# A perceiver kernel: cross attentions that begin with keys and scores, with the order of the absorbed attention, the phase features, the wide loads and the final norm changed too

## The reference

```python
# L0, L1 cross attention: 16 heads of 16
Q, K, V = heads(query @ Wq + bq), heads(ctx @ Wk + bk), heads(ctx @ Wv + bv)
x = x + merge(softmax(Q K^T / 4) V) @ Wo + bo            # L1 clamps the scores
# L0 attention: q and k get features of a phase
a = softplus(t); amp = a / sqrt(mean(a*a over the head) + 1e-6)
features = amp * sin(pi*tanh(p)), amp * cos(pi*tanh(p))  # those of q times lambda
# L2 cross attention: 8 heads of 64; L3 cross attention: one head of 256
# L3 feed-forward (mixture of 8 experts, top 2), the last step of all
src = src + moe(src); x = x + norm2_w * src / sqrt(mean(src*src) + 1e-6)
```

## Time and profile before

| | |
|---|---|
| time, median of 3 runs | 2164.79 us (2161.39 to 2168.08) |
| profiled execution, its own time | 2166.26 us |
| its span | 2164.5 us |
| PE busy | 1633.4 us (75%) |
| DVE busy | 1021.2 us (47%) |
| ACT busy | 732.4 us (34%) |
| POOL busy | 479.7 us (22%) |
| L0_xattn from, L0_attn's phase features | 28.4, 262.1 to 337.2 |
| L1_xattn from, L2's absorbed attention | 675.8, 1250.9 to 1451.3 |
| L3_xattn prepared from, run from | 1740.5, 1761.7 |

### The profile page before, as it was taken

How to read it: one execution, slowest core, us unless ns; L and a number is a source line. 1 busy time by engine, 2 the same in 40 slices (tenths; PEclk the granted TensorE clock), 3 DMA queues, 4 the chain that set the end, 5 groups by cost and what they waited for, 6 DMA issues and landing times. The chain is left out here.

```text
span 2164.5 us, 54009 instructions
## 1 busy us (share of the span) xinstructions
PE 1633.4 (75%) x21983; PEld 1404.8 (65%) x21983; DVE 1021.2 (47%) x2154; ACT 732.4 (34%) x1682; POOL 479.7 (22%) x634
## 2 busy tenths in 40 slices
PE   5998635769986999764888478867388968877684
PEld 4887534659974777654777367864277946655573
DVE  5655484241117888336111446554855734344314
ACT  3554331123333555221323245542223322332121
POOL 3442242002213343100444121200001200010241
PEclk9999755569997999765999789997697979676797
DMA  4110000049972111003999612210100153000584
GB/s 141 53 51 23 4 0 3 4 172 343 346 266 85 51 47 28 5 3 114 304 298 306 239 52 83 78 49 0 42 24 30 39 184 114 4 2 13 176 283 166
DMA packets 89649, 228.61 MB, mean 106 GB/s; under 512 B 20008, under 2 KB 42792, under 8 KB 81904
## 3 DMA queue, kind: packets, MB, share of 16 engines
q1 hardware_dynamic: 81296, 203.49, 28.5%
q0 software_dynamic: 8160, 22.29, 3.1%
HBM read 210.34 MB, written 15.34 MB: 104 GB/s over the span
## 5 line engine op out<-in xcount | busy, mean ns | idle before, releaser
L2215 PEld LDWEIGHTS ps<-xt,w 128*128 128x128 f32 x1728 | 212.6, 197 | 10.2 <-issue 4.0
L2215 PE MATMUL ps<-xt,w 128*128 128x128 f32 x1728 | 214.3, 281 | 2.5 <-DVE xt L2396 2.1
L2253 ACT ACTIVATE g<-ps,b 128x128 f32<-128x128 f32 x340 | 122.5, 367 | 272.7 <-PE ps L2215 253.0
L2225 PE MATMUL ps<-w,g 128*128 128x256 f32 x864 | 206.9, 388 | 0.0
L2225 PEld LDWEIGHTS ps<-w,g 128*128 128x128 f32 x864 | 160.7, 194 | 19.2
L2273 POOL DMA_INDIRECT x<-rows,token x85 | 83.3, 980 | 293.0 <-DVEq L2372 264.2
L2278 POOL DMA_INDIRECT results<-y,dest x85 | 83.7, 985 | 283.7 <-DVE y L2409 223.8
L2396 DVE COPY xt<-ps 128x256 f32<-128x256 f32 x85 | 36.1, 425 | 229.8 <-PE ps L2205 181.6
L472 PE MATMUL ps<-x,w 128*128 128x512 f32 x408 | 112.0, 433 | 19.5 <-DVE x L610 19.5
L454 PE MATMUL ps<-consts_sb,z_sb 128*128 128x128 f32 x176 | 41.3, 406 | 110.1 <-DVE z_sb L598 110.0
L454 PEld LDWEIGHTS ps<-consts_sb,z_sb 128*128 128x128 f32 x176 | 32.9, 210 | 119.9 <-DVE z_sb L598 116.6
(11 more groups left out here) (403 smaller groups left out, 3673.7 us busy)
## 6 DMA issues: line engine op xcount, KB each, us to landing
w<-in_L_ffn_w SPq DMA_DIRECT2D x124, 512.0 KB
w<-in_L_ffn_w SPq DMA_DIRECT2D x46, 1024.0 KB
c<-in_ctx SPq DMA_DIRECT2D x96, 258.0 KB, 2.8
b<-in_w_L_ffn SPq DMA_DIRECT2D x62, 128.0 KB
rows<-in_w_L_xattn SPq DMA_DIRECT2D x32, 192.0 KB
rows<-in_w_L_xattn SPq DMA_DIRECT2D x8, 768.0 KB
c<-in_w_L_xattn SPq DMA_DIRECT2D x8, 514.0 KB
back<-results SPq DMA_DIRECT2D x16, 256.0 KB, 5.2
```

The lines of the kernel that those rows point to most:

```text
L2215: mm = nc.tensor.matmul(hidden_bank(par, h), b.w1[:, par, c, h * P:(h + 1) * P], b.xt[:, par, c, :], start=c == 0, stop=c == DC - 1)
L2225: mm = nc.tensor.matmul(k.ps[:, YB + par, 0:D], b.g[:, par, h, :], b.w2[:, par, h, :], start=h == 0, stop=h == HC - 1)
L2253: nc.scalar.activation(b.g[:, par, h, :], hidden_bank(par, h), func, bias=b.b1[:, par, h:h + 1]).then_inc(s.g_ready, 1)
```

## The change

Six edits. In L0 and L1 cross attention PE makes keys, values and scores of batch 0 before the product of the tails; POOL orders the tails' columns after batch 0's split, DVE takes the first maxima before the values and before round_context(2), and bo is added to x in `prepare`. In the absorbed attention add_tails of a batch stands in that batch, before the split of the queries. The phase features leave POOL: ACT folds by Abs and squares, DVE multiplies sine and cosine by the amplitude first and by the norm from PSUM last. The context loads of L3_xattn are waited for slot by slot in the stage that uses them, and queries(i + 2) stand before outputs(i - 1). The last mixture norms, adds and stores tile by tile; `store_output` is gone.

```diff
+    for dst, src, done in ahead:
+        sp.dma_start(dst, src).then_inc(done, 16)
...
+                if raised is not None:
+                    dve.wait_ge(s.norm_done, NT)
+                    nc.vector.tensor_tensor(src[:], src[:], spread(raised, NT, 1), ALU.add)
...
-                if ahead:
+                if m:
...
+                    else:
+                        pe.wait_ge(s.tail_ready, 1)
...
+            pe.wait_ge(s.w_split, 2)
+            keys_values(0, 0, ahead=False)
+            scores(0, 0)
             pe.wait_ge(s.t_ordered, 2)
             for c, t in ((0, b.t0), (1, b.t1)):
                 kr = P if c == 0 else DK - P
-                last = nc.tensor.matmul(k.ps[0:B, 7, 0:D], t[:], w.wv[0:kr, c, :], start=c == 0, stop=c == 1)
+                last = nc.tensor.matmul(k.ps[0:B, OB, 0:D], t[:], w.wv[0:kr, c, :], start=c == 0, stop=c == 1)
             last.then_inc(s.tail_done, 1)
-            pe.wait_ge(s.w_split, 2)
-            keys_values(0, 0, ahead=False)
-            pe.wait_ge(s.tail_ready, 1)
-            scores(0, 0)
-            pe.wait_ge(s.values_ready, 1)
...
+            split_context(0)
+            spread_queries(0, 0)
             for t, ordered in ((given.t0, b.t0), (given.t1, b.t1)):
                 nc.gpsimd.tensor_copy(ordered[:].rearrange("p (b t) -> p b t", b=BT),
                                       t[:].rearrange("p (t b) -> p b t", b=BT)).then_inc(s.t_ordered, 1)
                 pool.wait_ge(s.t_ordered, 1 if ordered is b.t0 else 2)
-            split_context(0)
-            spread_queries(0, 0)
...
             round_context(1)
+            maxima(0, 0)
+            take_values(0, 0)
             round_context(2)
             dve.wait_ge(s.tail_done, 1)
             dve.wait_ge(s.ones_set, 2)
-            nc.vector.tensor_tensor(b.vtail[:, :, 0:16], k.ps[0:B, 7, 0:D].rearrange("p (h d) -> p h d", d=16),
+            nc.vector.tensor_tensor(b.vtail[:, :, 0:16], k.ps[0:B, OB, 0:D].rearrange("p (h d) -> p h d", d=16),
                                     w.bv[0:B, :].rearrange("p (h d) -> p h d", d=16), ALU.add).then_inc(s.tail_ready, 1)
-            take_values(0, 0)
-            maxima(0, 0)
-            nc.vector.tensor_tensor(k.x[:], k.x[:], spread(w.bo, NT, 1), ALU.add).then_inc(s.x_ready, 1)
-            dve.wait_ge(s.x_ready, 1)
...
-                        if not (begin and j == 0):
-                            add_tails(n - 1, (j + 1) % 2, group if j else group - 1, (j - 1) % BT)
                         if not final:
                             maxima(n + 1, (j + 1) % 2)
                         if not (end and j >= 2):
                             round_context(n + 2, j % 2, 4 * it + 2 * gpar + j // 2 + 1)
                         if not final:
                             reciprocals(n + 1, (j + 1) % 2)
+                        add_tails(n, j % 2, group, j)
...
-                dve.wait_ge(s.amp_done, u + 1)
-                nc.vector.tensor_tensor(b.f[:, u], amp[:, u], amp[:, u], ALU.mult).then_inc(s.square_done, 1)
...
+            dve.wait_ge(s.amp_done, 2)
+            dve.wait_ge(s.lam_done, 1)
+            for done, t in ((s.sin_done, sn), (s.cos_done, cs)):
+                dve.wait_ge(done, 1)
+                for c in range(DC):
+                    nc.vector.scalar_tensor_tensor(t[:, 0, c], t[:, 0, c], b.lam[:, 1, c:c + 1], amp[:, 0, c],
+                                                   ALU.mult, ALU.mult).then_inc(s.scaled, 1)
+                dve.wait_ge(done, 2)
+                nc.vector.tensor_tensor(t[:, 1], t[:, 1], amp[:, 1], ALU.mult).then_inc(s.scaled, 1)
+            for u in range(2):
                 dve.wait_ge(s.root_done, u + 1)
                 nc.vector.reciprocal(b.rms[:, 1, u], b.rms[:, 0, u]).then_inc(s.recip_done, 1)
+            dve.wait_ge(s.scaled, 6)
             for u in range(2):
                 for q in range(4):
                     dve.wait_ge(s.wide_done, 4 * u + q + 1)
-                    part = amp[:, u, q // 2, (q % 2) * 512:(q % 2) * 512 + 512]
-                    nc.vector.tensor_tensor(part, part, k.ps[:, 4 * u + q, :], ALU.mult).then_inc(s.norm_done, 1)
-            dve.wait_ge(s.norm_done, 8)
-            dve.wait_ge(s.lam_done, 1)
-            for done, t in ((s.sin_done, sn), (s.cos_done, cs)):
-                dve.wait_ge(done, 2)
-                for c in range(DC):
-                    nc.vector.scalar_tensor_tensor(t[:, 0, c], t[:, 0, c], b.lam[:, 1, c:c + 1], amp[:, 0, c],
-                                                   ALU.mult, ALU.mult)
-            nc.vector.tensor_tensor(cs[:, 1], cs[:, 1], amp[:, 1], ALU.mult)
...
-            for u in range(2):
-                nc.scalar.activation(ph[:, u], ph[:, u], ACT.Tanh).then_inc(s.tanh_done, 1)
+            nc.scalar.activation(ph[:, 0], ph[:, 0], ACT.Tanh).then_inc(s.tanh_done, 1)
             for u in range(2):
                 act.wait_ge(s.abs_done, u + 1)
                 nc.scalar.activation(amp[:, u], amp[:, u], ACT.Exp, scale=-1.0).then_inc(s.exp_done, 1)
+            nc.scalar.activation(ph[:, 1], ph[:, 1], ACT.Tanh).then_inc(s.tanh_done, 1)
+            for u in range(2):
+                act.wait_ge(s.tanh_done, u + 1)
+                nc.scalar.activation(cs[:, u], ph[:, u], ACT.Abs).then_inc(s.fold_done, 1)
             for u in range(2):
                 act.wait_ge(s.plus_done, u + 1)
                 act.wait_ge(s.rest_done, u + 1)
                 nc.scalar.activation(b.f[:, u], b.f[:, u], ACT.Ln).then_inc(s.ln_done, 1)
-            act.wait_ge(s.tanh_done, 2)
             act.wait_ge(s.const_done, 2)
             for u in range(2):
                 nc.scalar.activation(sn[:, u], ph[:, u], ACT.Sin, scale=PI).then_inc(s.sin_done, 1)
+            act.wait_ge(s.amp_done, 1)
+            nc.scalar.activation(b.f[:, 0], amp[:, 0], ACT.Square).then_inc(s.square_done, 1)
             for u in range(2):
                 act.wait_ge(s.fold_done, u + 1)
                 nc.scalar.activation(cs[:, u], cs[:, u], ACT.Sin, bias=b.half[:, 0:1], scale=-PI).then_inc(s.cos_done, 1)
+            act.wait_ge(s.amp_done, 2)
+            nc.scalar.activation(b.f[:, 1], amp[:, 1], ACT.Square).then_inc(s.square_done, 1)
...
-        @block.gpsimd
-        def _(pool):
-            nc.gpsimd.memset(b.eps[:], 1e-6).then_inc(s.const_done, 1)
-            nc.gpsimd.memset(b.half[:], PI / 2).then_inc(s.const_done, 1)
-            for u in range(2):
-                pool.wait_ge(s.tanh_done, u + 1)
-                nc.gpsimd.tensor_scalar(cs[:, u], ph[:, u], 0.0, 2.0, ALU.max, ALU.mult).then_inc(s.rise_done, 1)
-                pool.wait_ge(s.rise_done, u + 1)
-                nc.gpsimd.tensor_tensor(cs[:, u], cs[:, u], ph[:, u], ALU.subtract).then_inc(s.fold_done, 1)
-            pool.wait_ge(s.norm_done, 8)
-            pool.wait_ge(s.sin_done, 2)
-            nc.gpsimd.tensor_tensor(sn[:, 1], sn[:, 1], amp[:, 1], ALU.mult)
...
+            pe.wait_ge(s.root_done, 2)
...
+            if finish is not None:
+                for t in range(NT):
+                    sp.wait_ge(s.finished, t + 1)
+                    sp.dma_start(k.out[:, t], k.x[:, t]).then_inc(k.stored, 16)
+                sp.wait_ge(k.stored, 16 * NT)
...
+            if finish is not None:
+                for t in range(NT):
+                    act.wait_ge(s.summed, (t + 1) * top)
+                    if t:
+                        act.wait_ge(s.squared, t)
+                    nc.scalar.activation(fin.square[:], into[:, t, :], ACT.Square, scale=1.0 / 16,
+                                         accum_out=fin.mean[:, t:t + 1]).then_inc(s.squared, 1)
+                    if t % 4 == 3:
+                        act.wait_ge(s.squared, t + 1)
+                        if t == 3:
+                            act.wait_ge(s.eps_set, 1)
+                        nc.scalar.activation(fin.root[:, t - 3:t + 1], fin.mean[:, t - 3:t + 1], ACT.Sqrt,
+                                             bias=fin.eps[:, 0:1]).then_inc(s.rooted, 1)
...
+                def scale(t):
+                    if t % 4 == 0:
+                        dve.wait_ge(s.rooted, t // 4 + 1)
+                        nc.vector.reciprocal(fin.inverse[:, t:t + 4], fin.root[:, t:t + 4]).then_inc(s.inverted, 1)
+                        dve.wait_ge(s.inverted, t // 4 + 1)
+                    nc.vector.scalar_tensor_tensor(into[:, t, :], into[:, t, :], fin.inverse[:, t:t + 1], finish,
+                                                   ALU.mult, ALU.mult).then_inc(s.scaled, 1)
+
+                dve.wait_ge(s.summed, NT * top)
+                scale(0)
+                for t in range(NT):
+                    if t + 1 < NT:
+                        scale(t + 1)
+                    dve.wait_ge(s.scaled, t + 1)
+                    nc.vector.tensor_tensor(k.x[:, t, :], k.x[:, t, :], into[:, t, :], ALU.add).then_inc(s.finished, 1)
...
+                else:
+                    pe.wait_ge(k.context_ahead[i], 64 if i == 0 else 48)
...
```

(30 more changed lines are left out.)

37 lines of the change are left out of this document (18 added, 19 removed).

## The result

| | before | after |
|---|---|---|
| median | 2163.22 us (4 runs, 2161.39 to 2168.08) | 2105.44 us (4 runs, 2102.95 to 2111.83) |
| profiled execution, its span | 2166.26, 2164.5 us | 2102.95, 2101.1 us |
| ratio | | 0.9724 (0.9691 to 0.9757) |

The ratio is a gain of 59.7 us, the medians differ by 57.8; 52.2 was forecast, at 2113 with a range of 2104 to 2122. Two later measurements of the same kernel gave 2112.0 (0.9755) and 2102.66 (0.9713).

The account below looks back on a forecast made before the run. No one engine was taken to bound the kernel; each part was priced in its own stage. Terms -22.6 - 19.5 - 11.0 - 6.4 + 7.3 = -52.2 gave 2113 us; range 2104 to 2122, 8 in 10.

Parts of the forecast that it names:

- Phase features: L0_attn phase features: with POOL's work gone and DVE's products reordered, -22.6 us, bounds -18 and -24.
- Rival D: Phase features: the long DVE ops are not POOL's doing; 6.3 us later, 2119 us; chance 0.06.
- Absorbed attention: L2 absorbed attention: adding tails before the query split removes PE's 16 waits, -19.5 us, bounds -13 and -21.
- Rivals E and F: Absorbed loop: E, context loads take over waits, 2121 us, 0.06; F, tails' add waits on u, slower than before, 0.02.
- Wide loads: L3_xattn: loads waited for by batch group, queries start 11.6 us earlier, -11.0 us kept, bounds -8 and -12.
- rival C: L3_xattn wide loads bind harder: queue at 270 GB/s, end 2.8 us later, 2116 us; chance 0.08.
- The end: Final norm: squares on ACT under DVE's sums, smaller last store, -6.4 us, bounds -5 and -7.5.
- Cross starts: Starts of L0_xattn and L1_xattn: late tail DMAs delay load 4, +3.5 and +3.8, together +7.3 us, bounds +0.4 and +10.
- Rival B: Cross starts lose nothing, as load 4 lands in time or the loop has slack; 2106 us; chance 0.08.

Follow-up runs that it names:

- fold_act: Kernel before with only the phase's fold moved from GpSimd to one ACT Abs per tensor: 2147.04 us, ratio 0.9920.
- after_again: The changed kernel itself measured a second time, nothing altered: 2112.00 us, ratio 0.9755.
- cross_alone: Kernel before with only the edit of the L0 and L1 cross starts: 2172.86 us, ratio 1.0030.
- after_b: The changed kernel measured a third time, on one chip with three variants: 2102.66 us, ratio 0.9713.
- round_first: Changed kernel with round_context(2) moved ahead of the first maxima and values in the cross attentions: 2098.97 us, ratio 0.9721.
- the last set: One-chip runs: changed kernel 2102.66 us; with loads 4 and 5 ahead of tails 2098.40; with round_context(2) ahead too 2099.40; with old cross starts 2102.68.

## Why the forecast held in sign and mechanism, and where its sizes were off

**Phase features**: right in mechanism, -23.6 for -22.6. The first square was forecast 24.5 us into the stage and came at 24.1, the sums of squares end at 306.22 (38.0; I had 38.3). The last multiply ended 0.8 us sooner than in my sum, mostly because 16 of them take 9.7 us, not 10.3: 0.60 each from start to start. Rival D is out by fold_act.

**Absorbed attention**: right in mechanism, and the step of the forecast that failed by its size: -24.1 for -19.5, beyond its bound of -21. Both numbers in the term were wrong, in the same direction. "21.2 us in 16 pieces" is idle time up to a modelled end; from start to start, and with the slower transposes behind them, the pieces are worth 24.3. And "I give back 1.7" for a later context load did not happen: the load's wait is 1.6 to 3.6 us in the profiles without the edit and 1.7 to 3.6 in those with it. Rivals E and F are out.

**Wide loads**: -10.0 for -11.0, in its bounds. PE waits for the reloads 2.4 to 4.9 us in sum, in two to five pieces, against 1.4 to 2.8 without the edit: the DMA gives a part of the 11.6 back, somewhat more than the 0.4 that I had it take, and the window from 1710 to 1736 moves 300 GB/s at a share of 0.95, so the 270 of rival C did not come either. The full 11.6, which the forecast's estimate from the Trainium skill's figure of some 358 GB/s (SBUF — State Buffer, A bandwidth-pool intuition that's wrong) would have kept, did not come.

**The end**: -6.6 for -6.4 over all profiles, and partly by luck. The last addition came 6.4 us after the sums (I had 6.2), and the span ends 3.3 us after it, not 2.5: 9.7 us where I had 8.7. Against the one profile that the forecast was read from that is -5.5; but the kernel before takes 1 us more on average than in that profile, since its one store is done later in half of them. Why it is, no run shows.

**Cross starts**: +8.1 for +7.3, the right sum from two terms that were off in opposite ways, which is luck: +5.2 for +3.5 in L0, +2.8 for +3.8 in L1. The chain is the one that I wrote down, to the row: the wait of batch 4 on the DMA is 3.3 to 3.4 us in L0 in all four profiles. In L1 it is 3.7 in the first profile and 2.1 to 2.3 in the three others, so that term was too large. The rest is smaller: the scores of batch 0 let the maxima start 0.9 us sooner into the stage (I had 1.4), and the addition of bo makes the preparation 0.4 us longer in L0 and nothing in L1 (10 profiles with it, 8 without; I had 0.6 for each).

What was not in the term is TensorE's clock, which fell behind the hole. The kept traces give it a price. The hole lies between the scores of batch 2 and those of batch 3, which follow one another by 4.64 us in L0 of the kernel before:

| L0 | VectorE's wait | lower clock behind the hole | scores of batch 2 to 3 | beyond 4.64 and the wait |
|---|---|---|---|---|
| after | 3.27 | 6.7 | 10.07 | 2.2 |
| after_again | 3.30 | 6.7 | 9.94 | 2.0 |
| cross_alone | 3.42 | 6.7 | 10.06 | 2.0 |
| after_b | 3.36 | 3.3 | 9.22 | 1.2 |
| round_first | 1.65 | 3.3 | 7.45 | 1.2 |

The last column goes with the time at 1.2 GHz and not with the wait. And the same work, from a batch's first matmul of the keys to its scores, takes 5.96 us at the lower level and 3.68 at the upper one in the next batch, 2.3 us more. So in L0 the wait and the clock together make the 5.2, and the clock is the 1.7 that my term lacked. In L1 three of the four profiles fit (after_again and cross_alone: 6.7 us at the lower level, 1.9 us beyond the wait; after_b: none and 0.1), but in the first profile of the changed kernel 3.4 us at the lower level cost nothing. No run changed the clock and left the hole, so this rests on the comparison of traces. Rival B is out for the stages (cross_alone +6.5 us); in whole times the last set does not show it.

**The whole.** Terms as measured sum to -56.3, 4.1 from the forecast, and the absorbed attention alone is off by 4.6. By the forecast's own way of adding, -56.3 gives 2108.5 us, inside its range; the first measurement lay 3 us below that and the second (2112.0) 3.5 above. The three measurements lie at -59.7, -53.0 and -62.1 by their ratios; the stages that nothing touched do not differ between the kernels within their scatter, and the expert loop alone scatters by 9 us. What remains between -56.3 and their mean of -58.3 is well within that and stays unexplained.

**A better version.** The changed kernel with loads 4 and 5 ahead of the tails and round_context(2) ahead of the maxima: L0 212.3 and L1 223.2 us over three profiles, 1.0 and 1.9 below the mean of the profiles without the edit. Its times are 2098.89, 2099.40 and, with the swap undone, 2097.06, beside 2105.44, 2112.00 and 2102.66 of the changed kernel; on one chip the ratios are 0.9678 (0.9654 to 0.9702) and 0.9713 (0.9693 to 0.9733), which just overlap.

## What to carry to other kernels

Price a hole in PE's work by the distance of two starts, with and without it, and not by the idle column: here 1.51 and not 1.36 us, 14 times over, and 1.57 by the period of the loop. Before a producer is moved back, look at the queue whose next entry waits for it: the tails cost nothing by being late, the context loads behind them did, and sending two loads first mended both layers. A hole can also cost more than its length: behind this one TensorE's lower clock took 2 us more. Where a change moves 50 us and the scatter of one execution is 10, compare stage by stage over several profiles; single totals would have told of a gain of the last stage that is not there.

## What the runs showed of the hardware that was not expected

VectorE and GpSimd took strict turns on the 128x2048 tiles of the phase features: an operation's recorded time holds the rest of the other engine's operation and then, but for 0.15 us, its own. So the same addition shows 5.64 and 8.09 us in one trace, depending on how much of GpSimd's operation was left, and 1.23 when GpSimd is idle. I had priced it at 2.28, since the trace of before never shows it alone. The Trainium skill (SBUF — State Buffer, Who interferes with whom) says that tensor_scalar can enter a faster mode that takes both port pairs, and that this mode contends with GpSimd; 1.23 us, about half of the 2.29 for the same elements, and the 5.64 agree with that.

Behind a hole of 4 us in which PE was busy for 1.75 the granted clock stood at 0.50 for 6.7 us. In the same window, 51.3 to 58 us, three other profiles with the hole, which lies a little elsewhere in each, have 0.53, 0.59 and 0.75, and the 13 without it 1.00. After the shorter hole of round_first it stood at 0.51 for 3.3 us.
